# Halving the squares of the keys on GpSimd in the 20 steps that have no value product

## The reference, cut to what matters

```python
kh = (kv @ Wk).reshape(b, s, HEADS, HEAD_DIM).transpose(0, 2, 1, 3)
kh = rms_norm(kh, k_norm_w)     # x * rsqrt(mean(x*x over the 64) + 1e-5) * w
scores = jnp.einsum('bhld,bhsd->bhls', qh, kh) * (1.0 / np.sqrt(HEAD_DIM))
scores = jnp.where(mask, scores, NEG_INF)
attn = jax.nn.softmax(scores, axis=-1)
o = jnp.einsum('bhls,bhsd->bhld', attn, vh)
```

## Time and profile before

| | |
|---|---|
| median of the runs | 2514.92 us |
| profiled execution | 2512.21 us, its span 2510.1 us |
| granted TensorE clock, mean | 0.978 |
| busy: PE, DVE, ACT, POOL | 2324.6, 2173.2, 1328.5, 1404.8 us |
| steps 0 to 19 | from 147 to 228 us of the span, about 81 us |

### The profile page before, as it was taken

One profiled execution on the slowest core, in us unless ns is written; L12 is line 12 of the kernel. 1 busy time (PEld: TensorE's weight loads), 2 busy tenths in 40 slices (PEclk: granted clock), 3 DMA queues, 4 the chain that ended last, 5 costly groups with the idle time before them and its releaser, 6 DMA issues. The chain is left out here.

```text
span 2510.1 us, 57306 instructions
## 1 busy us (share of the span) xinstructions
PE 2324.6 (93%) x16359; PEld 1926.5 (77%) x16359; DVE 2173.2 (87%) x3384; ACT 1328.5 (53%) x2566; POOL 1404.8 (56%) x1021
## 2 busy tenths in 40 slices
PE   6878999999999999999999999999999998999842
PEld 3656888888888888888888888888888877776522
DVE  6789999999999999999999999999999995477657
ACT  5744555555555555555555555555555545355440
POOL 3413666666666666666666666666666660011155
PEclk9999999999999999999999999999999999999965
DMA  2431122222222222222222222222222216220000
GB/s 90 168 103 46 45 56 52 52 52 52 52 52 51 52 57 55 52 51 51 51 56 56 52 52 53 61 55 51 52 52 52 51 36 203 97 69 2 2 1 17
DMA packets 441099, 145.04 MB, mean 58 GB/s; under 512 B 365344, under 2 KB 423616, under 8 KB 440896
## 3 DMA queue, kind: packets, MB, share of 16 engines
q1 hardware_dynamic: 440880, 143.50, 23.1%
q10 hardware_dynamic: 144, 0.52, 0.1%
HBM read 109.17 MB, written 34.73 MB: 57 GB/s over the span
## 5 line engine op out<-in xcount | busy, mean ns | idle before, releaser
L450 POOL TENSOR_TENSOR probs<-arena,best_all 128x1024 f32 (+2 forms) x397 | 945.4, 2381 | 587.2 <-DVE best L815 538.6
L1058 PEld LDWEIGHTS u_ps<-rows,probs 128*128 128x128 f32 x6656 | 799.0, 191 | 80.5 <-issue 41.1
L1058 PE MATMUL u_ps<-rows,probs 128*128 (+1 forms) x6656 | 814.5, 276 | 22.3 <-ACT probs L646 18.5
L800 DVE SCALAR_TENSOR_TENSOR arena<-s_ps,mask,rrms 128x512 f32 (+2 forms) x832 | 603.9, 727 | 111.9 <-PE s_ps L936 109.2
L646 ACT ACTIVATE probs<-probs 128x1024 f32<-128x1024 f32 (+1 forms) x416 | 440.4, 1060 | 400.3 <-POOL probs L450 389.1
L776 DVE TENSOR_REDUCE ssq<-squares 128x16 f32<-128x1024 f32 (+1 forms) x416 | 501.2, 1205 | 25.0 <-ACT squares L604 25.0
L815 DVE TENSOR_TENSOR best<-best,arena 128x1024 f32<-128x1024 f32 (+1 forms) x352 | 499.5, 1419 | 0.1
L604 ACT ACTIVATE squares<-k_ps 128x512 f32<-128x512 f32 (+1 forms) x832 | 451.5, 591 | 54.4 <-DVE ssq L776 28.0
L934 PE MATMUL k_ps<-w_hi,cT_hi 128*128 128x512 f32 (+1 forms) x832 | 362.5, 436 | 10.8 <-ACT squares L604 10.5
L598 ACT ACTIVATE cT_hi<-cT 128x128 fp32r<-128x128 f32 (+1 forms) x416 | 129.2, 311 | 419.5 <-DVE cT L771 418.5
L934 PE MATMUL s_ps<-q_hi,cT_hi 128*128 (+2 forms) x832 | 333.6, 401 | 12.2 <-DVE row_sb L833 9.5
(11 more groups left out here) (224 smaller groups left out, 2076.1 us busy)
## 6 DMA issues: line engine op xcount, KB each, us to landing
stage<-in_ctx SPq DMA_DIRECT2D x1536, 16.0 KB, 1.7
rows<-in_ctx SPq DMA_DIRECT2D x32, 768.0 KB
queries<-probs SPq DMA_DIRECT2D x16, 1024.0 KB, 4.0
q_plain<-queries SPq DMA_DIRECT2D x32, 512.0 KB, 3.4
best_all<-best_rows SPq DMA_DIRECT2D x31, 512.0 KB, 3.7
u_transposed<-uT_sb SPq DMA_DIRECT2D x124, 128.0 KB, 2.6
a_uT<-u_transposed SPq DMA_DIRECT2D x10, 1024.0 KB, 4.8
arena<-u_transposed SPq DMA_DIRECT2D x6, 1024.0 KB, 5.0
```

The costliest lines, as they stand in the source:

```text
L450: pool.tensor_tensor(probs[0:r, slot_of(c, PRING), :], scores_at(b, c), best_all[0:r, bass.ds((b % 2) * HL, HL)], ALU.subtract).then_inc(s ...
L800: dve.scalar_tensor_tensor(out=scores_at(p, c, h * HALF, HALF).rearrange("p (h l) -> p h l", l=L), in0=s_ps[h][0:r, :].rearrange("p (h l) ...
L1058: last = pe.matmul(u_ps[g // 3][:, at:at + UW], probs[0:r, s, g * P:(g + 1) * P], rows, start=(c == 0 and g % 3 == 0), stop=(c == NC - 1), ...
```

## The change

In steps 0 to 19, GpSimd adds the upper 32 squares of each head to the lower 32, in place in `squares`, once both halves are written (`fold_squares`). VectorE then waits for GpSimd (semaphore `halved`) in place of ScalarE, and sums 32 values a head. All other steps are as before. GpSimd's new instruction stands behind `split_lo` and ahead of `split_q_lo` and `shift` of the same step.

```diff
+def no_values(p, c):
+    return isinstance(p, int) and 0 <= p * NC + c < NC + LAG
...
+            def fold_squares(n, c):
+                by_head = squares[0:rows_of(c), :].rearrange("p (h d) -> p h d", d=HD)
+                pool.wait_ge(squared.sem, squared.ended(n + KEYS_AHEAD))
+                low, high = by_head[:, :, 0:HD // 2], by_head[:, :, HD // 2:HD]
+                pool.tensor_tensor(low, low, high, ALU.add).then_inc(halved, 1)
...
+                if on.keys and no_values(p, c):
+                    fold_squares(n, at_step(p, c, KEYS_AHEAD)[1])
...
-            def sum_squares(n, c):
+            def sum_squares(n, c, folded=False):
                 r = rows_of(c)
-                dve.wait_ge(squared.sem, squared.ended(n))
-                dve.tensor_reduce(ssq[0:r, c * H:(c + 1) * H], squares[0:r, :].rearrange("p (h d) -> p h d", d=HD),
+                if folded:
+                    dve.wait_ge(halved, n - KEYS_AHEAD + 1)
+                else:
+                    dve.wait_ge(squared.sem, squared.ended(n))
+                width = HD // 2 if folded else HD
+                dve.tensor_reduce(ssq[0:r, c * H:(c + 1) * H],
+                                  squares[0:r, :].rearrange("p (h d) -> p h d", d=HD)[:, :, 0:width],
                                   AX_X, ALU.add).then_inc(summed.sem, 1)
```

More of the change, by code:

```diff
@@ L290, in cross_attention @@
         squared = Turns(sem("squared"), CREDIT, 2)
-        ssq_clear = sem("ssq_clear")
+        ssq_clear, halved = sem("ssq_clear"), sem("halved")
         summed = Turns(sem("summed"), CREDIT)
@@ L886, in step @@
                 if on.keys:
-                    sum_squares(n + KEYS_AHEAD, at_step(p, c, KEYS_AHEAD)[1])
+                    sum_squares(n + KEYS_AHEAD, at_step(p, c, KEYS_AHEAD)[1], no_values(p, c))
                 if on.rows and c == 1 and not draining(p):
```

## The result

The changed kernel has a median of 2509.27 us over 11 runs (2504.96 to 2514.56), the kernel before 2516.63 over 11 (2512.08 to 2519.88). The ratio is 0.9973 with a 95% interval of 0.9963 to 0.9982: about 7 us less, 4.5 to 9.3. The time forecast was 2509.2, from a median of before of 2514.92; the later runs of before lifted that by 1.7 us. The gain forecast was 5.7 us and the difference of the medians is 7.4; both lie inside the interval. That the time comes out within 0.1 us of the forecast is luck: the base was 1.7 us higher than the one from which it was taken, and the gain by the medians 1.7 us larger.

What follows compares the result with a forecast made beforehand. VectorE was taken to bound steps 0 to 19 and TensorE the rest. Step terms summed to 5.65 us at the first value product, 5.7 at the end, so 2514.92 would become 2509.2 us; range 2504.5 to 2514.5.

Steps and rivals of the forecast that it cites:

- What bounds the stretch: Steps 0 to 19: VectorE sets the pace, TensorE from step 20; time won counts once, at the first value product.
- 2 to 9: Plain steps: each sum 0.53 us shorter with the addition hidden and no slack left; 4.2 us gained over eight steps.
- the first shift: Steps 18 and 19: the last addition stands ahead of GpSimd's shift, starting it 1.28 us later than otherwise; -0.75 us net.
- The addition's length: GpSimd's addition of 512 pairs a row: 1.28 us, from a line through 128 and 1024 pairs; bounds 0.98 and 2.38.
- Step 14: No running maximum between two sums, so VectorE waits 1.09 us for the addition and sums 0.53 faster: -0.55 us.
- Steps 10 and 11: q_lo, delayed by an addition, stalls step 11's maximum instead of step 10's, by 1.9 us; two shorter sums gain 1.0.
- the edge on which a further 1.3 hung: Step 11: if its addition too gets in before the running maximum, 1.3 us goes, leaving -0.3.
- Step 15: Addition starts 0.06 us ahead of the running maximum, which loses 1.1 us: -0.55; +0.53 if VectorE wins.
- Step 17: Norm's small steps push the maximum into a tie with the addition; taken as won, 0.53 us, or -0.55 if lost.
- The slow addition: Rival: an addition of 2.38 us makes plain steps 4.33 us and the kernel 13 us slower, 2528; chance of slower 0.07.
- The mild ring: Rival: at 1.6 us, squares, addition and sum bind; a plain step gains 0.23, total about 0, 2514.5 us; chance 0.15.
- the gain does not pass on: Rival: a transfer or the start of the values holds the first value product; 2514.9 us or 0.8 more; chance 0.10.

Runs made afterwards that it cites:

- the run with the memset: Changed kernel with a GpSimd memset of 128x256, some 0.3 us, ahead of each addition; 2507.95 us in one execution.
- the run of the short sum: Changed kernel without GpSimd's additions, the upper 32 squares of each head left out and VectorE waiting for ScalarE; 2505.02 us in one execution.
- the run with the waits: Changed kernel, but in steps 15 and 17 GpSimd's addition also waits for that step's running maximum; 2510.08 us in one execution.
- its variant: Kernel before with one wait added: in step 10 GpSimd makes q_lo only after that step's running maximum; 2513.18 us in one execution.

## Why the prediction was right

**What bounds the stretch, and that the gain goes through to the end.** Right. VectorE set the pace; from the second value product on the two first profiles are equal within 0.3 us over 1858 us, and all thirteen within 0.6.

**The terms, one by one.** Forecast, and measured in the first and second profile of the changed kernel against the first of the kernel before, from the starts and ends of sums and maxima after the first scaling:

| steps | forecast | first | second |
|---|---|---|---|
| 0, 1 | +0.2 | +0.23 | |
| 2 to 9 | +4.2 | +4.27 | |
| 10, 11 | +1.0 | +1.31 | |
| 12, 13 | +1.05 | +1.06 | |
| 14 | -0.55 | -0.56 | |
| 15 | -0.55 | -0.54 | |
| 16, 17 | +1.05 | -0.07 | +1.08 |
| 18, 19 to the first value product | -0.75 | -1.59 | -1.24 |
| sum | 5.65 | 4.11 | 5.62 |

Where the last column is empty, the second profile's sums start within 0.03 us of the first's. That the second column comes to 5.6 like the forecast is luck in part: steps 10 and 11 gave 0.3 more than said and the first shift 0.5 less, and the two cancel. The first column is 1.5 below it.

**The addition's length.** 1.28 from a line through two rows, 1.29 measured. The forecast hung on this choice between bounds of 0.98 and 2.38, and the run with the memset shows how much: 0.05 us of slack, and behind it the rest of the delay shows in every plain step.

**Step 14**, in which VectorE has no maximum and must wait: 1.09 forecast (a wait, with the release of VectorE in it); the profile of the changed kernel has

```profile
198.67 0.71 DVE L818 SCALAR_TENSOR_TENSOR arena<-s_ps,mask,rrms 128x512 f32<-128x512 f32 x1
200.26 0.69 DVE L793 TENSOR_REDUCE ssq<-squares 128x16 f32<-128x512 f32 x1 [0.88 <-POOL squares L491]
```

0.88 of idle time and the rest in the start of the instruction.

**Steps 10 and 11.** The number was near, the mechanism not quite as forecast. On VectorE:

```profile
185.30 1.63 DVE L800 TENSOR_SCALAR ms<-ssq 128x128 f32<-128x128 f32 x1
186.85 1.49 DVE L833 TENSOR_TENSOR best<-best,arena 128x1024 f32<-128x1024 f32 x1
```

and on GpSimd:

```profile
184.47 2.38 POOL L485 TENSOR_TENSOR q_lo<-q_plain,q_hi 128x1024 fp32r<-128x1024 f32 x1
186.81 0.46 POOL L496 TENSOR_TENSOR cT_lo<-cT,cT_hi 128x128 fp32r<-128x128 f32 x1
187.22 2.27 POOL L491 TENSOR_TENSOR squares<-squares 128x512 f32<-128x512 f32 x1
```

It is the small `mean_squares` (0.23 us in the kernel before) that stands behind q_lo, not the maximum; the maximum then loses 0.27 to the subtraction and wins against the addition, which takes 2.27. I had foreseen a maximum of over 3 us in step 11 and had left `mean_squares` out, which VectorE runs ahead of it. The price came out 0.3 smaller, and the edge on which a further 1.3 hung was won.

**Step 15** as forecast. The rule of the Trainium skill ("SBUF — State Buffer", section "Who interferes with whom"), that the first to issue holds the pair, agrees with it: GpSimd first by 0.06 or 0.07 us in each of the three profiles and in that without the addition of step 19, and VectorE stands. It agrees with the run of the short sum too, in which VectorE was first by 0.24, and with the earlier trace rows. It does not fit the case of step 17, where GpSimd's instruction starts 0.01 or 0.02 us ahead in the same four profiles and loses in three, nor the second pair of the earlier trace rows. So the order of the starts in the profile does not always tell who gets the port; why, no run here shows.

**Step 17** was called a tie and taken as won. It is one: lost in the first profile and won in the next two. The term is worth +0.53 or -0.61, and which of them a run gets is luck.

**The first shift** is the term that I mis-sized. The late start by one addition was right: by the forecast the shift starts 5.39 - 0.53 + 1.28 = 6.14 us behind the maxima, and in the run with the waits, which has no slow piece up to there, it is 6.08. The changed kernel took 7.00, 6.64 and 6.57. What was not in the sum is the clock. TensorE, in the profile of the changed kernel around steps 15 and 18:

```profile
205.22 0.50 PE L952 MATMUL s_ps<-q_hi,cT_hi 128*128 128x512 f32 x1 [1.86 <-DVE arena L818]
...
207.94 0.63 PE L953 MATMUL k_ps<-w_lo,cT_hi 128*128 128x512 f32 x1
...
216.46 0.71 PE L952 MATMUL s_ps<-q_hi,cT_hi 128*128 128x512 f32 x1 [3.47 <-DVE row_sb L851]
216.97 0.63 PE L953 MATMUL s_ps<-q_lo,cT_hi 128*128 128x512 f32 x1
```

A matmul starts 0.23 us after the one before at the full clock and 0.43 at the lower one. TensorE had stood idle 1.86 and 3.47 us ahead of these pieces. The scores of step 19 (second and third profile) or 18 (first) came late for it: VectorE waited 1.02 us for them in the second, 0.84 in the first, and the squares that the last addition waits for were late as well. That took -0.75 to -1.24 and -1.59. The row of the second profile:

```profile
220.07 0.75 DVE L818 SCALAR_TENSOR_TENSOR arena<-s_ps,mask,rrms 128x512 f32<-128x512 f32 x1 [1.02 <-PE s_ps L954]
```

I had checked whether TensorE could keep the pace, and not whether it would keep its clock while it waited.

The fall behind step 15 goes with the collision. All four profiles with that collision (three of the changed kernel and the one without the addition in step 19) have 1.85 or 1.86 us of idle time of TensorE there and a slow piece that starts within 2.2 us of its end. The nine without it, the four of the kernel before and its variant among them, have 0.29 to 0.80 us of idle time at the same place and no slow piece between steps 15 and 17. With the waits the row of the first matmul behind the maximum is

```profile
202.98 0.50 PE L954 MATMUL s_ps<-q_hi,cT_hi 128*128 128x512 f32 x1 [0.79 <-DVE arena L820]
```

Taking the collision away took the slow piece away, then, in all five variants that do it. The fall in step 18, which is the one that held the shift, is not settled: the kernel before has 2.90 us of idle time there and no fall in two of three profiles, and among the variants with 2.35 to 2.40 us two fell and three did not. So the idle time by itself does not decide it.

**The rivals.** The slow addition (13 us lost) needed more than 1.83 us of it; it is 1.29. The mild ring is what the run with the memset makes: the addition ends 0.27 us later, as if it took 1.56. I had put the gain at about 0 for 1.6 us, and 3.8 us of it remained (81.02 - 77.18): a plain step lost 0.22 and not 0.3, and the later addition no longer collides in step 15. That the gain does not pass on was ruled out by the equal rest.

**The chance and the size.** The medians say 7, the middle part 5.3. The parts ahead of the stretch differ by up to 4 us from run to run (first scaling at 147.3 to 151.3 in the profiles, by the same instructions), and those behind it by as much. Five us of difference in the middle are inside the interval of 4.5 to 9.3; where the other 2 come from, if they are anything, no run here shows. The three profiled executions of the kernel before (2512.21, 2513.11, 2513.63) all lie 3 us or more under its median of 2516.63, so no profile shows what such a run holds.

## What to carry to other kernels

When an engine is given a part of another's sum, write the ring of waits with a time at each arrow (here squares 1.09, addition 1.29, sum 0.67 and the latencies) and see whether it is shorter than the pace of the bound engine; here they were equal within 0.05 us, and 0.27 us more in the ring took 0.22 off the gain of each plain step. Then go through the irregular steps one at a time: eleven plain steps brought 5.9 us, and steps 14, 15, 17 and the first shift took 3.3 back in the first profile. Take the new work out of the steps in which it gains nothing, and have it wait where it would start just ahead of an instruction that excludes it. And where executions of one kernel differ by more than the change is worth, measure between two fixed instructions in several profiles.

## What the runs showed of the hardware that I had not expected

- Two instructions that exclude each other at the port between VectorE and GpSimd, started 0.02 us apart, go either way from run to run: 1.29 and 2.35 us, or 2.35 and 1.22. Of four profiles with GpSimd 0.01 or 0.02 us ahead it won one. With GpSimd 0.06 or 0.07 us ahead it won in four of four; with VectorE 0.19 or 0.24 us ahead VectorE did.
- The loser stands until the other is over, whoever it is: q_lo took 3.25 instead of 2.38 behind a maximum begun 0.24 earlier, the small `mean_squares` 1.63 instead of 0.23 behind q_lo.
- A GpSimd addition over two strided halves, 16 runs of 32 values, took 1.29 us, where the line through the flat forms of 128 and 1024 pairs gives 1.28. No run has 512 flat pairs. With 65 partitions instead of 128 it is 1.27 or 1.28.
- The lower TensorE clock lasted 3 to 4 us at a time in the stretch, after idle times of TensorE between 1.85 and 3.47 us, and came in 9 of 13 profiles, at places that shift with small changes. It moves a result of this size by up to 1.7 us (0.7 in the kernel before, 1.65 in the run with the waits, and nothing where the shift waits for the reload anyway), so one profile of each kernel is too few for it.
